# Routing each tile inside the main loop and scattering its rows into room per expert, in place of a placement stage after it

## What is computed

```
x = x + xattn(layernorm(x), ctx)       # q and k normalised per head, 16 heads of 16
x = x + attn(layernorm(x))             # scores += lambda * tanh(Q) J tanh(K)^T, causal
h = layernorm(x)
shared = (silu(h @ shared_gate) * (h @ shared_up)) @ shared_down
probs = softmax(h @ router_w); topk_probs, topk_idx = top_k(probs, 2)
for e in experts: routed += (silu(h @ gate[e]) * (h @ up[e])) @ down[e] * coeff[:, e]
out = x + routed + shared
```

## Time and profile before

| | before |
|---|---|
| median of 3 runs | 1490.43 us (1487.72 to 1491.38) |
| the profiled execution's own time | 1506.31 us |
| its span, first to last instruction | 1504.5 us |
| TensorE busy in the span | 1265.3 us (84%) |
| VectorE busy | 989.1 us (66%) |
| ScalarE busy | 667.6 us (44%) |
| GpSimd busy | 436.5 us (29%) |
| mean transfer rate | 54 GB/s |

### The profile page before, as it was taken

How to read it: one execution, slowest core, us unless ns; L and a number is a source line. 1 busy time by engine, 2 the same in 40 slices (tenths; PEclk the granted TensorE clock), 3 DMA queues, 4 the chain that set the end, 5 groups by cost and what they waited for, 6 DMA issues and landing times.

```text
span 1504.5 us, 56188 instructions
## 1 busy us (share of the span) xinstructions
PE 1265.3 (84%) x22760; PEld 1038.9 (69%) x22761; DVE 989.1 (66%) x2206; ACT 667.6 (44%) x1234; POOL 436.5 (29%) x436
## 2 busy tenths in 40 slices
PE   4699999999999999999999999999997448999200
PEld 3577877777777787878787777878875347778100
DVE  5557777777777777777777777777764395555333
ACT  0245555555555555555555555555553101444000
POOL 1212222222222322222222222222211003555465
PEclk9889999999999999999999999999999656999655
DMA  4600000001100000010011000000100002556555
GB/s 143 192 20 24 27 27 31 27 27 34 41 27 27 27 27 27 27 31 27 27 33 41 27 27 27 27 27 27 31 10 12 12 0 67 152 152 150 144 174 167
DMA packets 67119, 80.73 MB, mean 54 GB/s; under 512 B 8176, under 2 KB 59504, under 8 KB 66928
## 3 DMA queue, kind: packets, MB, share of 16 engines
q1 hardware_dynamic: 60016, 58.84, 12.5%
q0 software_dynamic: 6912, 18.88, 5.1%
HBM read 54.62 MB, written 23.07 MB: 52 GB/s over the span
## 4 chain that ended last, share of the span: by engine, by line
PE 57%; DVE 16%; issue 12%; DMA 6%; POOL 4%; ACT 2%; SPq 2%; DVEq 0%; POOLq 0%; ACTq 0%
PE ringB L434 12%; PE ringC L445 11%; PE oA L527 5%; PE banksS L510 5%; DMA ct_in<-in_ctxT 4%; PE banksS L474 4%; DVE mx L1120 3%; PE banksS L727 3%; POOL pt L986 2%; PE ringB L608 2%; PE oA L434 2%; PE ringB L594 2%; PE banksS L700 2%; DVE mx L1166 2%; DVE sc L1172 2%
## 5 line engine op out<-in xcount | busy, mean ns | idle before, releaser
L804 ACT ACTIVATE pt<-banksS 128x1024 f32<-128x1024 f32 x128 | 127.6, 1023 | 119.4 <-PE banksS L510 112.4
L445 PE MATMUL ringC<-wx_kv,ct 128*128 128x256 f32 x512 | 159.6, 312 | 11.0 <-POOL ct_rest L951 7.4
L1120 DVE TENSOR_REDUCE mx<-banksS 128x8 f32<-128x2048 f32 x64 | 146.7, 2293 | 14.0 <-PE banksS L489 14.0
L951 POOL TENSOR_TENSOR ct_rest<-ct_in,ct 128x1024 fp32r<-128x1024 f32 x32 | 75.6, 2362 | 269.4 <-DVE ct L1064 269.4
L445 PE MATMUL ringC<-wx_kv_rest,ct 128*128 128x256 f32 x512 | 147.4, 288 | 0.0
L445 PE MATMUL ringC<-wx_kv,ct_rest 128*128 128x256 f32 x512 | 147.3, 288 | 0.0
L510 PE MATMUL banksS<-qT,kT 17*128 17x64 f32 x4096 | 133.1, 279 | 0.9 <-DVE qT L1125 0.9
L510 PEld LDWEIGHTS banksS<-qT,kT 17*128 17x128 f32 x4096 | 124.2, 192 | 8.0 <-issue 1.4
L956 POOL TENSOR_TENSOR sc<-sc,rz 128x1024 f32<-128x1024 f32 x32 | 61.0, 1905 | 195.7 <-DVE rz L1181 195.7
L445 PEld LDWEIGHTS ringC<-wx_kv,ct 128*128 128x128 f32 x512 | 99.9, 195 | 19.5 <-issue 8.5
L986 POOL DMA_INDIRECT pt<-normalised_rows,ids x80 | 75.8, 947 | 128.9 <-DVE ids L1345 70.9
(11 more groups left out here) (220 smaller groups left out, 2972.6 us busy)
## 6 DMA issues: line engine op xcount, KB each, us to landing
ct_in<-in_ctxT SPq DMA_DIRECT2D x64, 256.0 KB, 2.9
expert_rows<-kc SPq DMA_DIRECT2D x80, 128.0 KB
xt<-in_x SPq DMA_DIRECT2D x32, 128.0 KB, 2.0
normalised_rows<-h SPq DMA_DIRECT2D x32, 128.0 KB, 1.8
rows_without_experts<-base SPq DMA_DIRECT2D x32, 128.0 KB, 1.7
kT<-rows_without_experts SPq DMA_DIRECT2D x32, 128.0 KB
out<-ksq SPq DMA_DIRECT2D x32, 128.0 KB
...
```

Of the source, the lines that this page charges most:

```text
L445: mm = pe.matmul(ringC[:, half * DIM:(half + 1) * DIM], left[:, p, k, j // 2, (j % 2) * P:(j % 2 + 1) * P], right[:, k, part * DIM:(part + ...
L804: act.activation(pt[:, g, :, :, :, :].rearrange("p i q c n -> p i (q c n)"), banksS[:, :, g * 256:(g + 1) * 256], ACT.Exp)\
L951: pool.tensor_tensor(ct_rest[:, p, :, :, :], ct_in[:, :, :, :], ct[:, p, :, :, :].bitcast(F32), ALU.subtract).then_inc(ev["ct_rest_ready"] ...
L1120: dve.tensor_reduce(mx[:, 2 * r:2 * r + 2, :, HD].rearrange("p q i -> p i q"), banksS[:, :, :].rearrange("p i (q m) -> p i q m", q=2), AX. ...
```

## The change

Routing moves into the loop and the placement stage goes.

- **Order.** The pipeline gets one more step (`LAGS` is 6 with the second scatter). The context of a tile is split at lag 0, its K0 product and its statistics come at lag 1, keys, queries and values at lag 2, cross attention at 3, self attention at 4, feed-forward at 5. The order of all parts on all engines and the turns of the accumulation banks are new. GpSimd's steps are written out.
- **SP** loads the context of tile s first and the rows x of tile s - 1 behind it. The store of h is gone. The triangular matrix and the number table are loaded among the first weights.
- **Per tile** VectorE takes the maximum of the logits, ScalarE the exponential, VectorE the two best (`two_best`), TensorE the count of earlier rows per expert (`counts`, two small 16-bit products) and VectorE two row addresses (`rows_placed`). Each expert has room for all rows, and GpSimd scatters h to both addresses (`rows_scattered`; h has two buffers).
- **Zeros.** At the start SP writes 2 x 256 rows of zeros and more, nine transfers of 256 KB (`clear_rows`); near the end of the loop it writes 256 rows of zeros behind the rows of each expert, DRAM to DRAM at register addresses (`pad_experts`), before the last tile's scatter.
- **After the loop** VectorE makes two tables, for the first 16 and the other 64 slots: where the slot's rows and its weights lie. Then it scales the down weights. TensorE waits for all of it.
- **Experts.** SP reads the slot's address into a register and loads a plain block of 128 rows, and stores the result of eight slots before. The loops of TensorE, VectorE and SP are written out. VectorE turns the row addresses into result addresses in five ops between slots (`rows_found`). Combining is as before, with these addresses.

```diff
+ROOM = TOK + P
+FIRST_SLOTS = E
...
+LAGS = 6
+LEAD = 8
...
+            def clear_rows():
+
+                sp.wait_ge(setup_dve, 1)
+                sp.dma_start(zeros_d.rearrange("(p q) d -> p q d", q=2), h[:, :, :]).then_inc(zeros_out, 16)
+                for n in range(E // 2):
+                    at = E * ROOM + 2 * n * P
+                    sp.dma_start(rows_d[at:at + 2 * P, :].rearrange("(p q) d -> p q d", q=2), h[:, :, :]).then_inc(zeros_out, 16)
+
+            def pad_experts():
+
+                sp.wait_ge(zeros_out, 16 * (1 + E // 2))
+                sp.wait_ge(pads_known, 1)
+                for e in range(E):
+                    sp.reg_load(row_at[e % DEEP], pad_at[0:1, e:e + 1])
+                    at = sp.snap(row_at[e % DEEP], min_val=0, max_val=E * ROOM - 2 * P)
+                    sp.dma_start(rows_d[bass.ds(at, 2 * P), :], zeros_d[:, :]).then_inc(pads_out, 16)
...
             def step(s, odd):
-                on(s, odd, 0, load_rows)
-                on(s, odd, 4, store_rows)
+                if isinstance(s, int) and s == TILES - 1 + 5:
+                    pad_experts()
                 on(s, odd, 0, load_context)
-                on(s, odd, 4, store_base)
+                on(s, odd, 1, load_rows)
+                on(s, odd, 5, store_base)
+            row_at = [sp.alloc_register(f"row_at{c}") for c in range(DEEP)]
             load_cross_weights()
+            clear_rows()
             tiles(sp, step)
 
-            def store_y(j, c, n):
+            def load_slot(j):
+                c = j % DEEP
+                sp.wait_ge(slots_known, 1 if j < FIRST_SLOTS else 2)
+                if j >= DEEP:
+                    sp.wait_ge(ev["rows_turned"].sem, ev["rows_turned"].of(j - DEEP))
+                sp.reg_load(row_at[0], rows_at_i[0:1, j:j + 1])
+                at = sp.snap(row_at[0], min_val=0, max_val=E * ROOM + (E - 1) * P)
+                sp.dma_start(xg[:, c, :], rows_d[bass.ds(at, P), :]).then_inc(rows_in[c], 16)
+
+            def store_y(j):
+                c = j % DEEP
                 sp.wait_ge(ev["y_ready"].sem, ev["y_ready"].of(j))
-                sp.dma_start(block_of(y_t, j), y[:, c, :]).then_inc(y_out[c], 16)
-            rounds(sp, SLOTS, store_y)
+                sp.dma_start(y_d[j * P:(j + 1) * P, :], y[:, c, :]).then_inc(y_out[c], 16)
+
+            sp.wait_ge(pads_out, 16 * E)
+            for p in range(2):
+                sp.wait_ge(scattered[p], 16 * TILES)
+            for j in range(SLOTS + 2 * DEEP):
+                if j < SLOTS:
+                    load_slot(j)
+                if j >= 2 * DEEP:
+                    store_y(j - 2 * DEEP)
...
+            def counts(d, p):
+
+                claim(pe, C_USES, C_BANKS, "CNT", d)
+                pe.wait_ge(ev["sel_ready"].sem, ev["sel_ready"].of(d))
+                mm = pe.matmul(ringC[:, 0:E], before16[:, :], sel16[:, :], start=True, stop=False)
+                mm = pe.matmul(ringC[:, 0:E], ones16[:, :], earlier16[:, :], start=False, stop=True)
+                if isinstance(d, int) and d >= TILES - 2:
+                    mm = pe.matmul(ringC[:, E:2 * E], ones16[:, :], sel16[:, :], start=True, stop=False)
+                    mm = pe.matmul(ringC[:, E:2 * E], ones16[:, :], earlier16[:, :], start=False, stop=True)
+                mm.then_inc(full["CNT"].sem, 1)
 
...
+                on(s, odd, 3, rough_scores, 0)
+                on(s, odd, 4, self_rows_turned)
+                on(s, odd, 5, self_weighted, 0)
+                on(s, odd, 5, self_weighted, 1)
+                on(s, odd, 2, context_product, "K1", 1, 0)
+                on(s, odd, 5, self_output)
+                on(s, odd, 4, self_qk)
+                on(s, odd, 2, rows_turned)
+                on(s, odd, 3, rough_scores, 1)
+                on(s, odd, 2, query_product)
+                on(s, odd, 4, heads_turned, "TQ", 0)
+                on(s, odd, 4, heads_turned, "TK", 1)
+                on(s, odd, 3, maxima_turned)
+                on(s, odd, 5, ffn_rows_turned)
+                on(s, odd, 4, self_mix)
+                on(s, odd, 3, scores, 0)
+                on(s, odd, 5, route)
+                on(s, odd, 5, gate_and_up)
+                on(s, odd, 3, weighted, 0)
+                on(s, odd, 3, scores, 1)
+                on(s, odd, 3, weighted, 1)
+                on(s, odd, 2, context_product, "V0", 0, 1)
+                on(s, odd, 5, gated_turned)
+                on(s, odd, 4, self_scores)
+                on(s, odd, 3, weighted, 2)
+                on(s, odd, 4, self_values)
+                on(s, odd, 3, weighted, 3)
+                on(s, odd, 2, keys_turned)
+                on(s, odd, 3, cross_output)
+                on(s, odd, 5, counts)
+                on(s, odd, 5, down)
+                on(s, odd, 2, context_product, "V1", 1, 1)
+                on(s, odd, 4, probs_turned, 0)
+                on(s, odd, 2, queries_turned)
+                on(s, odd, 4, probs_turned, 1)
+                on(s, odd, 1, context_product, "K0", 0, 0)
...
+            pe.wait_ge(slots_known, 1)
             pe.wait_ge(weights_set, 3)
...
+            def routing_exponential(d, p):
+                act.wait_ge(ev["below_ready"].sem, ev["below_ready"].of(d))
+                freed(act, ev["sel_ready"], d)
+                act.activation(prob[:, :], below[:, :], ACT.Exp).then_inc(ev["prob_ready"].sem, 1)
+
...
+                on(s, odd, 3, exponential, 3)
+                on(s, odd, 5, gated_rows_in)
+                on(s, odd, 2, values, 0)
+                on(s, odd, 4, self_values_in)
+                on(s, odd, 4, self_exponential)
+                on(s, odd, 2, keys_in)
+                on(s, odd, 2, values, 1)
+                on(s, odd, 2, queries_in)
+                on(s, odd, 4, probs_in, 0)
...
+            def rows_scattered(d, p, k):
+
+                if k == 0:
+                    pool.wait_ge(ev["pos_ready"].sem, ev["pos_ready"].of(d))
+                if d == TILES - 1 and k == 0:
+                    pool.wait_ge(pads_out, 16 * E)
+                pool.indirect_dma_start(out=rows_d[:, :], out_offset=bass.IndirectOffsetOnAxis(ap=pos_u[:, 2 * d + k:2 * d + k + 1], axis=0),
+                                        in_=h[:, p, :], in_offset=None).then_inc(scattered[p], 16)
+
...
+                on(s, odd, 5, ffn_rstd)
+                on(s, odd, 4, self_biased)
+                on(s, odd, 2, keys_scaled, 1)
+                on(s, odd, 2, keys_scaled, 0)
+                on(s, odd, 6, rows_scattered, 1)
+                on(s, odd, 1, context_rest)
+                on(s, odd, 4, self_probs)
+                on(s, odd, 3, self_rstd)
+                on(s, odd, 5, rows_scattered, 0)
                 on(s, odd, 1, cross_biased)
+                on(s, odd, 1, cross_rstd)
+            for s in range(TILES + LAGS):
+                step(s, s % 2)
+            pool.wait_ge(slots_known, 3)
...
             def routing_logits(d, p):
                 dve.wait_ge(full["RT"].sem, full["RT"].of(d))
-                dve.tensor_copy(row(logits, d), bankB("RT")[:, 0:E]).then_inc(free["RT"].sem, 1)
+                freed(dve, ev["prob_ready"], d)
+                dve.tensor_reduce(top, bankB("RT")[:, 0:E], AX.X, ALU.max).then_inc(ev["top_found"].sem, 1)
+                after("top_found", d)
+                dve.tensor_scalar(below[:, :], bankB("RT")[:, 0:E], top, None, ALU.subtract).then_inc(ev["below_ready"].sem, 1)
+
+            def two_best(d, p):
+
+                dve.wait_ge(ev["prob_ready"].sem, ev["prob_ready"].of(d))
+                freed(dve, full["CNT"], d)
+                dve.tensor_reduce(m1, prob[:, :], AX.X, ALU.max).then_inc(ev["ranking0"].sem, 1)
+                dve.tensor_reduce(total, prob[:, :], AX.X, ALU.add).then_inc(ev["ranking1"].sem, 1)
+                after("ranking0", d)
...
+                here = coef[:, 2 * d:2 * d + 2] if isinstance(d, int) else coef[:, bass.ds(2 * d, 2)]
+                dve.tensor_scalar(here, best[:, 3:5], inverse, None, ALU.mult)
+                dve.tensor_tensor(sel16[:, :], hot[:, 0, :], hot[:, 1, :], ALU.add).then_inc(ev["sel_ready"].sem, 1)
+
+            def rows_placed(d, p):
+
+                dve.wait_ge(full["CNT"].sem, full["CNT"].of(d))
+                if isinstance(d, int) and d == TILES - 2:
...
+                    dve.tensor_scalar(per_int[:, 0, :], ringC[:, E:2 * E], P - 1.0, None, ALU.add).then_inc(table, 1)
+                    dve.wait_ge(table, 1)
+                dve.tensor_tensor(at_row[:, :], ringC[:, 0:E], room_at, ALU.add).then_inc(ev["placing0"].sem, 1)
+                dve.tensor_tensor(earlier16[:, :], earlier16[:, :], sel16[:, :], ALU.add)
+                after("placing0", d)
+                dve.tensor_tensor(hot[:, :, :], hot[:, :, :], at_row[:, :].unsqueeze(1).to_broadcast([P, 2, E]), ALU.mult).then_inc(ev["placing1"].sem, 1)
+                after("placing1", d)
```

(54 more changed lines are left out.)

380 lines of the change are left out of this document (123 added, 257 removed).

## The result

The changed kernel takes 1574.74 us (1565.25 to 1580.15), the kernel before 1489.54 (1487.72 to 1491.38): ratio 1.054, interval 1.051 to 1.058. I had forecast 1445. The profiled execution of the changed kernel has a span of 1578.3 us, 73.8 more than before's 1504.5.

A forecast was written before the change was run, and what follows sets the result against it. Four stages have four limits; in the loop, TensorE's busy share and a ring through VectorE. From 1506.3 us profiled: start +24, loop -19, loop end +4, routing gap -50, expert stage -5 give 1460; scaled to the median, 1445 us, range 1415 to 1490.

The forecast's parts named there:

- The start: Up to the first self maxima: zero writes and expert weights on SP's queue delay tile 1's rows x, +24 us.
- The loop: 30 steps of the main loop: from 34.42 to 33.8 us each, 19 us less in all.
- the ring: Dependent chain through TensorE, VectorE and ScalarE that sets the loop step; four terms sum to 33.4 to 34.2 us.
- the forecast's own sign: Loop: the forecast is wrong if the step is over 35.3 us, or SP's queue is solid in the expert stage.
- the VectorE term: Loop step, VectorE from the maximum of the logits to the shifted self scores: 11.5 us.
- the 8.5 us: Loop step before the change, VectorE from Newton steps to shifted self scores, 520.20 to 528.74; part of the 11.5.
- VectorE's chain sets the step: Loop rival: the added 3.9 us do not fit, step 36.2 us, loop +53, time 1516 us; chance 0.10.
- Scatters held up by VectorE: Loop rival: each step's scatters wait for two long VectorE ops, +56 us, time 1500 us; chance 0.03.
- The end of the loop: Last two steps: nothing hides VectorE's two-best chain and places, +4 us.
- The routing gap: Between loop and expert stage: old routing work goes, slot tables and down-weight scaling replace it, -50 us.
- SP or the pads bound the stage: Expert stage: SP takes 2.0 us a slot, 1472 us, chance 0.10; late pads delay tile 31's scatter, 1450 to 1460, 0.05.
- The tail: Combining stage after the experts: not changed in kind, left at its time, 0 us.

The follow-up runs named there:

- e4: Changed kernel with both edits of e3 and the expert-weight load moved from behind tile 2's context to behind tile 3's rows x: 1442.96 us.
- e1: Changed kernel with GpSimd's context_rest made to wait for the end of the two-best chain: 1475.62 us.
- e3: Changed kernel with the edit of e1, and the sum into earlier16 and three ops behind it moved behind the self-attention statistics: 1456.55 us.
- p1: Separate probe kernel, computing nothing of the reference: GpSimd ops beside VectorE ops; a scatter took 2.82 us beside the 4,096-column scaling, 1.03 beside a sum with a PSUM operand.
- b1: Kernel before with one line moved, GpSimd's context_rest behind the two keys_scaled: 1482.55 us, ratio 0.993.

## Why the prediction was wrong

**The start** was right in place and size: the key copy came at 78.47 (I had 80), TensorE's gap lay at 58 to 79, and e4 shows its cause. The split was less exact: moving the weights gives 22 us back at the first self maxima (I had 19), moving the zeros 2 (I had 5).

**The loop** is the step that failed. I forecast 33.8 us by walking the ring and laid VectorE's additions on it at the length of unhindered ops, 0.21 us each, 3.9 per tile. By the forecast's own sign, a step over 35.3 us, it is wrong. The ring was the right path, and three of its four terms came as forecast where the clock is full; the VectorE term came to 13.9 us instead of 11.5. Three of the 20 added ops read SBUF only and stand beside GpSimd instructions of 1 to 2.4 us. They brought 5.1 us of hold per step, and with the waits of TensorE came the lower clock. e1 and e3 give back 105 and 123 of the 132 us by which I missed the loop (113 + 19), in the same 30 steps of their traces. That the VectorE term is 11.5 again in e1 and e3 is in part luck: the 8.5 us that I took from the earlier trace rows had 1.0 us of hold in them, which the new order doesn't have, and the 11.5 us of e3 have 0.55 of hold and 0.4 of waiting for TensorE. The hint was in a row that I quoted: I took the 8.5 us from it and did not ask why 80 columns took 1.22 us in one op and 0.20 in the next.

**The rival "VectorE's chain sets the step"** had the right outcome (a step over 35.3 us, slower) and not the cause: with all 20 ops still there, e1 and e3 have steps of 34.7 and 34.1, so the ops fit and the holds did not. It was also too small, 36.2 against 38.2. **"Scatters held up by VectorE"** had the right pair of engines and the wrong one waiting; my argument against it, 0.94 us for gathers beside busy VectorE, holds in this kernel and not in general (p1).

**The end of the loop** came at +7 instead of +4; one held `earlier16` (1.85 us) is in it.

**The routing gap** went about as forecast: the first block is transposed 11.5 us behind the last sum (I had 13 to 18), released by the scaling of the down weights:

```profile
1352.54 0.66 PE L755 MATMUL banksS<-ident,pt 128*128 128x128 f32 x2 [11.56 <-DVE w_down L1392]
```

```profile
1321.64 15.37 SPq L405 DMA_DIRECT2D rows_by_expert<-zeros  x16
```

The row of SP's queue is the pads: 15.37 us for 16, as forecast, 0.96 each. In the trace's records of one pad the issue takes 0.50 us and the register read 0.28; the rest lies between them. The last scatter waited for the pads until 1341.22, some 1 us after its addresses were ready (1340.13), and this was hidden behind the slot tables. So the rivals that SP or the pads bound the stage fall: SP's queue has gaps, and a slot takes 135.34 / 80 = 1.69 us (I had 1.65 to 1.7).

**The tail** I left at its time; it was 10.7 us shorter. b1, which doesn't touch it, also has it at 90.6 us (1390.1 to 1480.7), and all the experiments lie between 90.0 and 90.8. So before's 101.15 most likely belongs to its profiled execution, and its excess makes up most of the 1% by which that one stood over the median. I had spread this 1% over the whole sum.
